# Graph network kernel: the first eight graphs' wide convolution tap by tap with raw weights, and a rewritten opening

## The reference

```python
h = relu(layernorm(x))
x = x + L0(h)                      # L0 below
h = relu(layernorm(x))
x = x + adj @ (h @ weight) + bias
# L0(h), all per graph, hc = h transposed (features x nodes):
c = relu(bn1(conv1(hc)))           # 1 tap, 128 -> 128
c = bn2(conv2(c))                  # 17 taps over the nodes, padding 8, 128 -> 128
x_conv = relu(c + hc).T
s = h @ w_se.T + b_se              # 3 coordinates a node
A = exp(-|s_n - s_m|^2) * adj
x_nmp = A @ relu(h @ w_msg.T + b_msg)
# a GRU cell: input [x_conv, x_nmp], state h, weights w_ih, w_hh
```

## Time and profile before

| | |
|---|---|
| median of 3 runs | 378.87 us (378.32 to 379.08) |
| the profiled execution: time, span of the core | 378.42 us, 376.5 us |
| busy over the span | PE 91%, PEld 83%, DVE 76%, ACT 55%, POOL 46% |
| granted clock of TensorE, mean | 0.964 |
| opening (0 to the gates of pair 0) | 65.6 us, PE busy 46.8 us |
| last step and ending, from 348.9 on | 27.6 us |

### The profile page before, as it was taken

One profiled execution on the slowest core, in us unless ns is written; L12 is line 12 of the kernel. 1 busy time (PEld: TensorE's weight loads), 2 busy tenths in 40 slices (PEclk: granted clock), 3 DMA queues, 4 the chain that ended last, 5 costly groups with the idle time before them and its releaser, 6 DMA issues.

```text
span 376.5 us, 6337 instructions
## 1 busy us (share of the span) xinstructions
PE 341.2 (91%) x2212; PEld 311.8 (83%) x2212; DVE 286.4 (76%) x737; ACT 208.7 (55%) x403; POOL 174.1 (46%) x140
## 2 busy tenths in 40 slices
PE   5758776979999999999999999999999999989864
PEld 5757776769998899889988999889988998989663
DVE  4596688797878997797879887889767987653572
ACT  1545733576854686548744785468645835262242
POOL 7763247212890179224951298118911594072022
PEclk9886889998999999999999999999999999999998
DMA  7700020000220013000310031001100010000001
GB/s 256 275 3 0 0 66 20 0 1 2 86 83 2 1 58 113 0 0 30 105 36 1 2 112 57 0 2 65 49 1 2 0 57 1 3 28 30 0 0 57
DMA packets 7951, 15.10 MB, mean 40 GB/s; under 512 B 1008, under 2 KB 1648, under 8 KB 7792
## 3 DMA queue, kind: packets, MB, share of 16 engines
q1 hardware_dynamic: 7632, 14.56, 11.1%
q10 hardware_dynamic: 288, 0.14, 0.1%
HBM read 10.50 MB, written 4.19 MB: 39 GB/s over the span
## 4 chain that ended last, share of the span: by engine, by line
issue 40%; POOL 28%; PE 13%; DVE 11%; ACT 5%; DMA 1%; SPq 0%; POOLq 0%; DVEq 0%; ACTq 0%
POOL rs L1161 3%; POOL ac L838 3%; POOL px L842 3%; POOL base L1213 3%; POOL x_ring L1203 3%; POOL base L1215 3%; POOL px L832 3%; POOL px L840 2%; POOL px L835 2%; POOL base L1219 2%; POOL rs L1156 2%; ACT hn L601 1%; DMA x_ring<-x_in 1%; DVE cx_lo L931 1%; DVE st L855 1%
## 5 line engine op out<-in xcount | busy, mean ns | idle before, releaser
L1161 POOL TENSOR_TENSOR rs<-ve,neg_half 128x4 f32<-128x4 f32 x16 | 16.1, 1009 | 103.8 <-DVE ve L972 103.8
L280 PE MATMUL pP<-cx_hi,conv_hi 128*128 128x256 f32 x176 | 54.4, 309 | 5.6 <-DVE cx_lo L931 5.6
L281 PE MATMUL pP<-cx_lo,conv_hi 128*128 128x256 f32 x176 | 52.0, 296 | 0.0
L282 PE MATMUL pP<-cx_hi,conv_lo 128*128 128x256 f32 x176 | 52.0, 296 | 0.0
L280 PE MATMUL pQ<-cx_hi,conv_hi 128*128 128x256 f32 x144 | 46.0, 319 | 2.7 <-issue 2.2
L281 PE MATMUL pQ<-cx_lo,conv_hi 128*128 128x256 f32 x144 | 43.2, 300 | 0.0
L282 PE MATMUL pQ<-cx_hi,conv_lo 128*128 128x256 f32 x144 | 43.1, 299 | 0.0
L1156 POOL TENSOR_TENSOR rs<-ve,neg_half 128x8 f32<-128x8 f32 (+1 forms) x9 | 14.9, 1656 | 56.5 <-DVE ve L862 56.5
L280 PEld LDWEIGHTS pP<-cx_hi,conv_hi 128*128 128x128 f32 x176 | 34.4, 195 | 6.0 <-DVE conv_lo L936 3.5
L931 DVE TENSOR_TENSOR cx_lo<-px,cx_hi 128x576 fp32r<-128x576 f32 x32 | 35.0, 1116 | 0.6 <-ACT cx_hi L590 0.6
L282 PEld LDWEIGHTS pP<-cx_hi,conv_lo 128*128 128x128 f32 x176 | 34.3, 195 | 0.0
(11 more groups left out here) (246 smaller groups left out, 1022.3 us busy)
## 6 DMA issues: line engine op xcount, KB each, us to landing
x_ring<-x_in SPq DMA_DIRECT2D x16, 256.0 KB, 2.6
adj_ring<-adj_in SPq DMA_DIRECT2D x16, 256.0 KB, 3.3
out<-x_ring SPq DMA_DIRECT2D x15, 256.0 KB, 2.0
work<-conv_in SPq DMA_DIRECT2D x1, 1088.0 KB, 7.5
x_ring<-gate_in SPq DMA_DIRECT2D x1, 576.0 KB, 7.9
out<-x_ring SPq DMA_DIRECT2D x2, 128.0 KB, 1.7
work<-bias_in SPq DMA_DIRECT2D x1, 132.0 KB, 7.4
early<-early_in SPq DMA_DIRECT2D x1, 129.5 KB, 2.9
```

The costliest lines, as they stand in the source:

```text
L280: pe.matmul(acc, w_hi, m_hi, start=start, stop=False)
L281: pe.matmul(acc, w_hi, m_lo, start=False, stop=False)
L282: return pe.matmul(acc, w_lo, m_hi, start=False, stop=stop)
L1161: pool.tensor_tensor(rs2[g % 2][:], ve2[g % 2][:], neg_half[:, 0:GG], ALU.pow).then_inc(rs2_set, 1)
```

## The change

- Pair 0's conv2 is made by `direct(tap)`: each of the 17 taps with its raw weight, into pQ (phases 0 and 2) and pP (1 and 3), no sums and differences. Its residual and bias come from `residual_phases` on ScalarE instead of `sums` on POOL. The nested scheme starts with pair 1; its semaphore counts are shifted (`cx_before`, `pre_before`).
- The weight parts are rounded and split in another order: taps 0 to 15 and 16 raw first, sums last. POOL makes the weight sums (`sum_phases`) behind `scale1([2, 3])` instead of ahead of everything.
- SP loads x(1) before `early`, and `late` behind x(4) (it was on ScalarE's queue).
- On POOL `scale1([0])` and `scale1([1])` move in among the batch-norm vectors, and `pre(pool, 1, k)` no longer waits for `pair_set`.
- `pairs(g)` is cut in `coordinates` and `pair_rows`, with two `sv` buffers.
- All four openings get a new order. `gate_lo` moves behind `sums_lo(3)` on VectorE; `normalise1([4, 5])`, `shift1([4, 5])`, `first(4)`, `first(5)` and all five splits of pair 1 move ahead of the gates of pair 0. Warm-up matmuls are spread as 15, 3 and 6 instead of 17 and 9.

```diff
-        W_PARTS = (taps(5, T16), taps(8, M12), taps(8, M21), taps(8, A0), taps(8, A2))
-        W_SUMS = (2, 2, 3, 0, 0)
+        W_PARTS = (taps(8, A0), taps(8, A2), taps(1, T16), taps(4, M22), taps(8, M12), taps(8, M21))
+        W_SUMS = (0, 0, 0, 2, 2, 3)
+        SLOT = (0, 2, 1, 3)
...
             load_x(0)
+            load_x(1)
             sp.dma_start(early[:], early_in).then_inc(early_loaded, 16)
-            load_x(1)
...
+            def direct(tap, start=False, stop=False):
+                w = T16 if tap == 16 else 4 * (tap % 4) + tap // 4
+                w_hi, w_lo = conv_hi[:, w * D:(w + 1) * D], conv_lo[:, w * D:(w + 1) * D]
+                ends = []
+                for e, bank in enumerate((pQ, pP)):
+                    at_even, at_odd = e + tap, e + 2 + tap
+                    slots = [SLOT[at_even % 4], SLOT[at_odd % 4]]
+                    if slots[1] == slots[0] + 1 and at_even // 4 == at_odd // 4:
+                        parts = [(bank[:], slice(slots[0], slots[0] + 2), at_even // 4)]
+                    else:
+                        parts = [(bank[:, 0:CG * QN], slice(slots[0], slots[0] + 1), at_even // 4),
+                                 (bank[:, CG * QN:], slice(slots[1], slots[1] + 1), at_odd // 4)]
+                    for acc, phases, at in parts:
+                        m_hi, m_lo = cx_hi[:, phases, :, at:at + QN], cx_lo[:, phases, :, at:at + QN]
+                        ends.append((pe.matmul(acc, w_hi, m_hi, start=start, stop=False),
+                                     pe.matmul(acc, w_hi, m_lo, start=False, stop=False),
+                                     pe.matmul(acc, w_lo, m_hi, start=False, stop=stop)))
+                return ends
...
             def split_hi(t, k):
+                if t > 1:
+                    have(act, f_done[CX_FILLS[k]], t - (CX_FILLS[k] == 2))
+                elif k in (1, 2):
+                    have(act, f_done[4], 1)
+            def split_hi_phases(e):
+                act.wait_ge(c1_set, 2)
+                act.activation(cx_hi[:, 2 * e:2 * e + 2], c1[:, 2 * e:2 * e + 2], ACT.Copy).then_inc(cxhi_set, 1)
+            def residual_phases(e):
+                act.wait_ge(hT_set, 2)
+                act.activation(base[e][:], own(0, e), ACT.Identity, bias=bn_b[:, 1:2]).then_inc((sumE_set, sumO_set)[e], 1)
```

More of the change, by code:

```diff
@@ L461, in opening @@
                 messages(0)
+                keep_clock(6)
                 pe.wait_ge(w_split, 1)
-                pe.wait_ge(cxlo_set, 1)
-                product(pP, 0, X22, four(M22, True))
+                pe.wait_ge(cxlo_set, 2)
+                direct(0, start=True)
+                direct(4)
+                direct(8)
                 messages(1)
+                direct(12)
+                direct(1)
+                direct(5)
                 rows_turn(0)
-                pe.wait_ge(w_split, 2)
@@ L468, in opening @@
[L468 to L474, removed]
+                direct(9)
+                x_turn(2)
+                direct(13)
+                rows_turn(1)
+                distances(0)
+                pe.wait_ge(w_split, 2)
+                direct(2)
@@ L475, in opening @@
+                conv1(2)
                 distances(1)
[L476 to L479, removed]
                 messages(2)
                 x_turn(3)
+                direct(6)
+                neighbour_sums(0)
+                direct(10)
+                conv1(3)
                 neighbour_sums(1)
-                pe.wait_ge(s1_set, 1)
-                product(pP, 0, X32, four(M32)).then_inc(f_done[2], 1)
@@ L497, in opening @@
                 distances(3)
                 neighbour_sums(2)
-                product(pP, 1, X33, four(A3)).then_inc(f_done[4], 1)
+                direct(15)
                 neighbour_sums(3)
+                pe.wait_ge(w_split, 3)
+                even, odd = direct(16, stop=True)
+                even[2].then_inc(f_done[3], 1)
+                odd[0].then_inc(f_done[0], 1)
+                odd[1].then_inc(f_done[1], 1)
+                odd[2].then_inc(f_done[4], 1)
                 for g in range(2):
@@ L688, in scaled_third @@
             def scaled_third(t):
-                have(act, f_done[2], t + 1)
+                have(act, f_done[2], t)
                 have(act, sumO_set, t)
@@ L883, in hidden_lo, with coordinates, pair_rows @@
                    .then_inc(hlo_set, 1)
+            def coordinates(g):
+                have(dve, ms_done, g + 1)
+                dve.tensor_copy(sv[g % 2][:, :, 0:S], ms[:, :, D:MS]).then_inc(s_set, 1)
             def pairs(g):
+                coordinates(g)
+                pair_rows(g)
+            def pair_rows(g):
                 halves = svx[:].bitcast(F32)
@@ L1227, in opening @@
             def opening():
-                pre(pool, 0, 1)
-                pre(pool, 0, 2)
+                pool.wait_ge(cxlo_set, 2)
                 scale1([2, 3])
-                pre(pool, 0, 3)
-                pre(pool, 0, 4)
-                pre(pool, 0, 5)
-                sums(0)
-                pool.wait_ge(pair_set, 4)
+                sum_phases()
                 for k in range(1, 6):
```

230 lines of the change are left out of this document (117 added, 113 removed).

## The result

The kernel with the change takes **381.49 us** (median of six runs, 381.3 to 382.07); the kernel before, run beside it, takes 378.6 (six runs, 376.71 to 379.98). The ratio is **1.0094**, 95% interval 1.0069 to 1.0119: slower by about 0.9%, where +1.8 us (0.5%) was forecast. The profiled execution has a span of 379.7 us against 376.5, so 3.2 us more.

What follows compares the result with a forecast made beforehand. TensorE was taken to set the pace once the pipeline runs. Mark +3.6, clock +1.5 and first step -3.3 gave +1.8 us on the median of 378.87, so 380.7 us; 8-in-10 range 376.9 to 384.2.

Steps and rivals of the forecast that it cites:

- The chain through `gate_lo`, the load of x(5), the statistics and `first`: Opening: these queued operations hold back gates_c(0), which starts at 73.5 instead of 69.9, +3.6 us.
- the clock's term: After TensorE's long idle gap, some 3 us at half speed in gates_c(0) and gates_h(1): +1.5 us.
- the way to `neighbour_sums(3)`: TensorE's opening from 15.9: 24.0 us of taps, 10.2 of other work, 2.2 of stalls, ending at 52.3.
- the mark: Start of gates_c(0), the first matmul reading the convolution's result: 69.91 before, forecast at 73.5, +3.6 us.
- the first step's 3.3 us: Step 1: first(4), first(5) behind candidate(0) made TensorE wait; done before gates(0), the step falls from 43.8 to 40.5.
- gate_split to the mark: Opening, from gate_split at 56.1 through load, statistics, rs, first, splits and conv_out to gates_c(0) at 73.5: 17.4 us.
- (a): Opening: POOL's weight sums slow pair_rows(1) on VectorE, so distances(0) waits 0.5 us.
- (b): Opening: left_rows(2) is queued on ScalarE behind messages(3) and a round_w, so distances(2) waits 0.4 us.
- (c): Opening: pre(pool, 1, k) runs on top of pair_rows(3), so rows_turn(3) waits 1.3 us.
- No stall: Rival: no stall before neighbour_sums(3), which ends at 50.1; -0.4 us, 378.5 us, no change; chance 0.22.
- Faster, gate_lo sooner: Rival: a shorter head and no POOL collisions put gate_split at 52.3; -2.0 us, 376.9 us; chance 0.17.
- Collisions are worse: Rival: POOL's sums and differences hit more opening operations, gate_split at 58.5; +4.9 us, 383.8 us; chance 0.13.

Runs made afterwards that it cites:

- 2, with 52 fillers: The changed kernel with 52 identity matmuls into a free bank between gates_n(0) and gates_c(0): 379.84 us, ratio 1.0042.
- Experiment 1: The changed kernel with gate_lo moved on VectorE from behind split_w(5) to behind masked(0): 377.48 us, ratio 0.9984.
- experiment 3: The changed kernel with first(4) and first(5) put back behind candidate(0) on ScalarE: 377.81 us, ratio 0.9995.
- experiment 5: First kernel: the changed kernel with gate_lo behind masked(0) and first(4), first(5) behind candidate(0) together: 374.19 us, ratio 0.988.
- its second kernel: The first kernel of experiment 5 with normalise1([4, 5]) behind the last conv_lo_out and shift1([4, 5]) behind blend_start(0): 370.39 us, ratio 0.9783.
- 6: On top of its second kernel, sums_lo(3) and the splits (1, 3) and (1, 4) back behind the convolution's result: 368.8 us, ratio 0.9755.
- the best version: Experiment 5's first kernel, reordered: normalise1([4, 5]) in VectorE's idle stretch, POOL differences after pair_set 4, first(4) ahead of sums_hi(3), among other moves: 364.91 us, ratio 0.9648.
- 8: The best version with direct(6), direct(10) and direct(14) left out, so its output lacks these taps for eight graphs: 364.23 us, ratio 0.9628.
- 4: The changed kernel with direct(3), direct(7) and direct(11) moved behind neighbour_sums(3) on TensorE: 382.42 us, ratio 1.0122.
- the kernel with 33 fillers: The changed kernel with 33 identity matmuls into a free bank between gates_n(0) and gates_c(0): 380.81 us, ratio 1.0069.

## Why the prediction was right, and where it was off

The chain through `gate_lo`, the load of x(5), the statistics and `first` was right, step by step, and so was the clock's term. Two sizes in it were off, the way to `neighbour_sums(3)` (0.9 us too short) and the way from there to the mark (0.5 too long), and they partly cancel, which is luck. The reason given for the first step's 3.3 us was incomplete.

| Term | forecast | measured | where shown |
|---|---|---|---|
| first direct matmul | 15.9 | 15.99 | profile after |
| `neighbour_sums(3)` ends | 52.3 | 53.2 | profile after |
| gate_split | 56.1 | 57.2 | profile after |
| gate_split to the mark | 17.4 | 16.9 | profile after |
| landing of x(5) | 2.6 | 2.8 from issue, 2.86 of wait | profile after |
| mark | +3.6 | +4.2 | profile after |
| clock | +1.5 | +1.6 | 2, with 52 fillers |
| rest of step 1 | -3.3 | -3.1 | 39.5 against 38.0 - 1.6 |
| sum at pair 1's gates | +1.8 | +2.7 | profile after |

**The way to `neighbour_sums(3)`** was forecast with 34.2 us of work and 2.2 of stalls. From 16.00 to 53.20 TensorE was busy for 35.67 us and idle for 1.53. So the stalls were overrated and the work underrated. Part of the latter can be read off: 512-column matmuls of neighbouring rows follow each other by 0.235 us at 16.77 to 17.25 and by 0.255 us at 17.48 to 17.99, at the same granted clock; at 0.255 the 48 wide ones would cost 0.8 us more than at my 0.238, which is an upper end, since some run at 0.235. The rest of the 1.5 us stays open. Of the three stalls, (a) did not happen, (b) was 0.37, (c) 0.94. The collisions behind (a) did: a cast and a subtraction of 16 columns took 1.06 and 2.32 us beside the sums (0.17 us each beside no GpSimd operation, at 53.86 and 54.07 in the kernel before), as the timeline of VectorE has it, with GpSimd's below; TensorE had taps enough to cover them.

```profile
24.10 1.06 DVE L955 CAST svx<-sv 128x16 fp32r<-128x16 f32 x1
25.20 2.32 DVE L957 TENSOR_TENSOR svx<-sv,svx 128x16 fp32r<-128x16 f32 x1
```

```profile
25.09 2.40 POOL L1260 TENSOR_TENSOR work<-work 128x1024 f32<-128x1024 f32 x1
```

The Trainium skill (SBUF — State Buffer, section SBUF: two separate sides) calls the port pair that the two engines share an exclusive lock, held for a whole instruction, between a GpSimd operation that reads this memory and, among others, a VectorE operation with two inputs from it. The second row is such a one and ends 0.03 us behind GpSimd's, which agrees.

**From gate_split to the mark** I had 17.4 us; it is 57.24 to 74.10, 16.9. The load took 0.2 more than the 2.6; rs took 1.8 instead of 2.1, and conv_out to the second `xc_lo` 4.2 instead of 4.7 (69.86 to 74.10). The prediction also has 2.6 us as an estimate by the Trainium skill (DMA: Bandwidth & Descriptors, section Anatomy of one DMA); that section gives its fit for transfers issued by GpSimd. These three go over SP's queue, with a median of 3.1 us here. Experiment 1 shows that gate_lo in the chain costs 4.2 us, experiment 3 that `first(4)`, `first(5)` cost 3.7, experiment 5 that they give 7.6 together, and its second kernel that statistics and rs cost another 3.5. With all of them out of the way the mark lies at 62.9, near the 61 which the prediction named as the far end.

**The first step.** The size, -3.3, held (-3.1); the reason covers only a part of the mechanism. "first(4) and first(5) sat between candidate(0) and the gates of group 1" brings no wait in 3, nor with the statistics behind the result in 5. It takes a late `candidate(0)` as well: when `sums_lo(3)`, the statistics and the two splits all stand between `xc_lo` and the first blend, `h_lo` of group 4 is as late as in the kernel before (13.4 against 13.3 us behind the mark, 6), and the wait is 1.22 instead of 2.56 us only because TensorE itself comes 1.4 us later at the slow clock. That -3.3 came out is no proof of the reason: it was taken as the whole difference between two measured lengths, 43.8 and 40.5. That the step has no wait left at full clock is shown by the kernel with 52 fillers (36.4 us from mark to gates, 0.35 of wait).

**The rest.** The forecast's +1.8 against +2.7 at the gates of pair 1 is the mark's 0.6, the clock's 0.1 and 0.2 of step 1. The forecast's own range is given as 379.7 to 382.8; by its sum, gate_split at 54.9 and 58 give 379.5 and 382.6. The spans differ by 3.2. The windows of the last 19.5 us, of the kernel after and then of the one before, have a granted clock of 0.69 against 0.91, and in them the last group's second layer comes to be 3.0 us late instead of 2.7 (its first product at 373.24 against 370.24). Why the clock differs there isn't shown.

```profile
360.20:379.70 19.50, 12.21 (x64) 10.63 (x62) 8.61 (x26) 6.71 (x14) 4.52 (x4) 0.69 0.08 28
```

```profile
357.00:376.50 19.50, 11.13 (x66) 9.78 (x64) 10.13 (x28) 6.71 (x14) 4.52 (x4) 0.91 0.08 28
```

**Rivals.** "No stall" fell with the row at 53.23. "Faster, gate_lo sooner" described a true mechanism which the change did not set off; experiment 1 set it off by hand, with 377.48 us at a mark of 69.90, where the prediction had 376.9 for 69.7. "Collisions are worse" fell: 1.53 us of idle time in all. What speaks for the change is what the prediction had as "12 us earlier, spent in waiting": with another order on VectorE, ScalarE and GpSimd the same convolution gives 364.91 us. What the nested scheme would give in an order worked out as closely wasn't tried, so how much of these 13.5 us the direct form itself is worth stays open.

## What to carry to other kernels

When a rewritten stage ends early, look at what stands in the in-order queue between its result and its reader: here 12.6 us of the next pair's preparation, in pieces that lay in waits or behind the result in the old order. Ask of every operation that frees a buffer (gate_lo) which load waits for it, and place it by that load's date, not by its own reader's. Price a wait in the order with its whole queue: two backlogs that are each hidden can be visible together, and one long hole costs the clock on top. And before a missing wait is taken as proof, see whether the engine that should wait came late itself: a slow clock hid 1.4 us of one here.

## What the runs showed that I had not expected

- Taps that fill gaps are nearly free: the direct form has 9.7 us more work by the prediction's count, and taking 4.7 us out of the best version gave 0.4 to 0.7 (8), while moving them out of the gaps made the kernel 0.9 us slower than the change itself (4), with the clock at 0.50 from 46 to 52.
- The clock stayed at 1.00 through 52 fp32 products of the 128-column identity, each two records 0.114 us apart; the kernel got 1.6 us faster for work whose result nobody reads.
- The same wait of 2.40 us for `gate_lo` left the clock at 0.50 behind it in the kernel after (58 to 60) and at 1.00 in the kernel with 33 fillers (57 to 60). Up to there the two have the same order, so the cause isn't in it; what it is isn't shown.
- The kernel before scatters from 376.2 to 380.9 us in the 24 runs beside experiments 1 to 4; the one after spans 0.8 us in six. Part of it goes with the mean granted clock: the four runs above 380 us have 0.949 to 0.959, the five below 376.8 have 0.968 or 0.973. Why the clock differs between them isn't shown.
